# An audio tower's split into high and low halves: the fp16 high part written by ScalarE's second gelu pass instead of VectorE's cast

## The reference, cut to what matters

```python
CONV_LAYERS = [(128, 10, 5), (128, 3, 2), (128, 3, 2), (128, 3, 2), (128, 3, 2), (128, 2, 2)]
def _block(x, cw, cb, gw, gb, stride):
    y = lax.conv_general_dilated(x, cw, (stride,), 'VALID', ...) + cb[None, :, None]
    yg = y.reshape(B, NUM_GROUPS, C // NUM_GROUPS * T)
    mu, var = yg.mean(axis=-1, keepdims=True), yg.var(axis=-1, keepdims=True)
    yn = ((yg - mu) * lax.rsqrt(var + EPS)).reshape(B, C, T)
    return jax.nn.gelu(yn * gw[None, :, None] + gb[None, :, None])
h = x[:, None, :]
for (cw, cb, gw, gb), (_, _, s) in zip(conv_params, CONV_LAYERS):
    h = _block(h, cw, cb, gw, gb, s)
```

## Time and profile before

| what | us |
|---|---|
| median of 3 runs (from 1814.69 to 1819.27) | 1816.24 |
| the profiled execution | 1816.93 |
| its span, first to last instruction | 1815.3 |
| busy: TensorE matmuls, weight loads | 1464.7, 1019.8 |
| busy: VectorE, ScalarE, GpSimd | 1034.3, 754.8, 348.8 |
| mean granted clock of TensorE | 0.892 of full |

### The profile page before, as it was taken

How to read it: one execution, slowest core, us unless ns; L and a number is a source line. 1 busy time by engine, 2 the same in 40 slices (tenths; PEclk the granted TensorE clock), 3 DMA queues, 4 the chain that set the end, 5 groups by cost and what they waited for, 6 DMA issues and landing times.

```text
span 1815.3 us, 32241 instructions
## 1 busy us (share of the span) xinstructions
PE 1464.7 (81%) x10013; PEld 1019.8 (56%) x10014; DVE 1034.3 (57%) x2346; ACT 754.8 (42%) x1456; POOL 348.8 (19%) x390
## 2 busy tenths in 40 slices
PE   4975699998864899989747999898559999159997
PEld 3433477784433677753325777743347778137775
DVE  5987445558884445578964545598744546212221
ACT  2654355525642455435624555265435552012231
POOL 2000134300001334100002333000013331512111
PEclk7987699998986999989878999899769999579999
DMA  4300121210000221110002121100024332621110
GB/s 104 112 1 1 35 60 43 59 36 12 1 1 5 64 59 43 35 38 1 1 1 59 44 59 43 39 1 1 1 57 108 85 86 69 209 56 47 48 50 17
DMA packets 105852, 81.31 MB, mean 45 GB/s; under 512 B 57842, under 2 KB 96267, under 8 KB 105747
## 3 DMA queue, kind: packets, MB, share of 16 engines
q1 hardware_dynamic: 99988, 70.65, 15.5%
q0 software_dynamic: 5760, 9.36, 1.7%
HBM read 34.66 MB, written 18.38 MB: 29 GB/s over the span
## 4 chain that ended last, share of the span: by engine, by line
issue 50%; PE 30%; POOL 7%; DMA 4%; SPq 3%; DVE 3%; ACT 2%; POOLq 0%; DVEq 0%; ACTq 0%
PE ps L1649 5%; PE ps L1591 5%; PE ps L1802 4%; DMA arena<-arena 3%; PE ps L1635 3%; PE ps L1623 3%; PE ps L1782 2%; PE ps L1783 2%; POOL arena L765 2%; PE ps L1598 1%; POOL slot_scratch L824 1%; POOL arena L767 1%; SPq L587 1%; ACT arena L911 1%; PE ps L1790 1%
## 5 line engine op out<-in xcount | busy, mean ns | idle before, releaser
L1695 PE MATMUL ps<-arena,cwt 128*128 128x504 f16 (+2 forms) x1776 | 396.3, 387 | 62.1 <-DVE arena L1154 61.8
L1695 PEld LDWEIGHTS ps<-arena,cwt 128*128 128x128 f16 x1776 | 181.1, 104 | 268.3 <-DVE arena L1154 69.2
L1176 DVE TENSOR_REDUCE nmax<-ps 128x1 f32<-128x128 f32 (+5 forms) x288 | 176.9, 614 | 195.7 <-PE ps L1626 195.7
L1649 PE MATMUL ps<-arena 128*128 128x64 f32 (+2 forms) x2016 | 260.1, 269 | 9.1 <-DVE arena L1184 5.0
L1649 PEld LDWEIGHTS ps<-arena 128*128 128x128 f32 (+2 forms) x2016 | 241.9, 189 | 26.0 <-issue 17.8
L1156 DVE TENSOR_TENSOR arena<-arena 128x1008 f16<-128x1008 f32 (+4 forms) x200 | 227.0, 1135 | 6.9
L1184 DVE COPY arena<-ps 128x512 f32<-128x512 f32 (+4 forms) x288 | 156.1, 542 | 85.8 <-PE ps L1635 81.4
L893 ACT ACTIVATE arena<-ps,nmax 128x128 f32<-128x128 f32 (+5 forms) x288 | 180.8, 628 | 44.1 <-DVE nmax L1176 43.3
L1623 PE MATMUL ps<-arena 128*128 128x512 f16 (+6 forms) x780 | 164.6, 314 | 42.4 <-DMA arena<-arena 21.5
L1635 PE MATMUL ps<-ident,arena 128*128 128x128 f32 (+2 forms) x1008 | 165.8, 282 | 10.6 <-ACT arena L934 5.7
L950 ACT ACTIVATE arena<-ps 128x1008 f32<-128x1008 f32 (+1 forms) x112 | 96.3, 867 | 179.4 <-PE ps L1695 179.4
(11 more groups left out here) (249 smaller groups left out, 2060.5 us busy)
## 6 DMA issues: line engine op xcount, KB each, us to landing
arena<-arena SPq DMA_DIRECT2D x96, 187.5 KB, 3.0
arena<-arena SPq DMA_DIRECT2D x96, 93.8 KB, 2.6
slot_scratch<-empty_slot SPq DMA_DIRECT2D x1, 5775.0 KB, 19.1
arena<-in_L_ffn_w SPq DMA_DIRECT2D x8, 576.0 KB
arena<-in_L_ffn_w SPq DMA_DIRECT2D x8, 384.0 KB
arena<-slot_scratch SPq DMA_DIRECT2D x31, 96.5 KB, 1.9
arena<-slot_scratch SPq DMA_DIRECT2D x31, 96.0 KB, 2.0
xa<-in_x POOLq DMA_DIRECT2D x5, 468.8 KB, 4.3
```

The source lines that it names most:

```text
L1176: v.reduce_max(nmax[0:m, k_:k_ + 1], slot(g)[0:m, 0:128 * i + m], AX.X, negate=True).then_inc(S["smax_done"], 1)
L1649: last = t.matmul(slot(g)[0:m, Z_AT:Z_AT + DH], probt[k % 2][0:kk, c, 0:m], vt[0:kk, c, DH * hh:DH * hh + DH], start=c == 0, stop=c == i)
L1695: last = t.matmul(bank(g, k)[:, 0:c * PITCH].rearrange("p (r c) -> p r c", c=PITCH), cwt[layer][:, w, tap, :], parts[x][:, f:f + 2 * c - 1 ...
```

## The change

ScalarE makes the high part itself. For each piece of layer 0 and each chunk of layers 1 to 4 it now runs the gelu twice on the same source: first with the fp16 high part as its destination, then as before, to float32. VectorE's cast goes; it waits for ScalarE's `hi_done` and only subtracts. For a piece ScalarE waits for the low part only of the piece four earlier. Layer 5 has no split and stays. At the end of each batch ScalarE runs the tower's gelu on one column of ones.

```diff
-                for rows in NORM_CHUNKS[layer]:
+                for piece, rows in enumerate(NORM_CHUNKS[layer]):
...
+                    else:
+                        a.activation(split_views(layer, piece)[1], src, ACT.Gelu_apprx_tanh, bias=affine[:, 1:2],
+                                     scale=affine[:, 0:1]).then_inc(S["hi_done"], 1)
                     a.activation(dst, src, ACT.Gelu_apprx_tanh, bias=affine[:, 1:2], scale=affine[:, 0:1]
                                  ).then_inc(S["norm_done"], 1)
...
-                            wait(act, "hi_done", TOWER, SPLITS.index(had_it) + 1, b)
                             wait(act, "lo_done", TOWER, SPLITS.index(had_it) + 1, b)
                         src = slot(g).rearrange("p (m n) -> p m n", m=2)[:, :, 0:4 * PITCH]
+                        a.activation(split_views(0, piece)[1], src.rearrange("p m (k c) -> p m k c", c=PITCH),
+                                     ACT.Gelu_apprx_tanh, bias=affine[:, 1:2], scale=affine[:, 0:1]
+                                     ).then_inc(S["hi_done"], 1)
                         a.activation(stage[:, piece % STAGES, :].rearrange("p (m n) -> p m n", m=2), src,
...
+                a.activation(spare[:, 30:31], ones_col[:, :], ACT.Gelu_apprx_tanh)
...
-                n = SPLITS.index(unit) + 1
-                v.tensor_copy(high, src).then_inc(S["hi_done"], 1)
-                dve.wait_ge(S["hi_done"], at("hi_done", TOWER, n, b))
+                dve.wait_ge(S["hi_done"], at("hi_done", TOWER, SPLITS.index(unit) + 1, b))
                 v.tensor_tensor(low, src, high, ALU.subtract).then_inc(S["lo_done"], 1)
```

## The result

The changed kernel took 1913.66 us (median of 4 runs, 1913.17 to 1914.6) against 1815.92 for the kernel before beside it: 1.0536 times as long, 95% interval 1.0518 to 1.0554. The forecast was 1902, with a range from 1870 to 1932. The profiled execution took 1914.6 us, span 1912.6.

The account below looks back on a forecast made before the run. TensorE was taken to set the pace in the first two layers, with VectorE nearly full; later stages end with the last statistic. The parts sum to +21.4 us a batch, 85.6 in four, giving 1902 us, range 1870 to 1932.

Parts of the forecast that it names:

- Part one: First two layers, run together: second passes make ScalarE the bound instead of TensorE; +6.5 us a batch.
- The bound: First two layers: ScalarE replaces TensorE as the bound, and the 24 casts leaving VectorE give nothing.
- The price of the pass: Each added fp16 gelu of 1008 columns costs the same as the fp32 one: 1.08 us from PSUM, 1.12 from SBUF.
- part two: Layer 1 into 2: 26 passes leave TensorE without slots for 9.7 us, plus 1.9 us lost clock; +10.4 us a batch.
- Rival (b), the gate: First two layers: TensorE's short waits bring its clock to the lower level; +41 us a batch, 2066 us, chance 0.06.
- Parts three to five: Layers 2 into 3, 3 into 4 and 4 into 5: +3.3, +1.3 and -0.1 us a batch.
- Part six: Dummy gelu at batch end: its table load falls in idle time, the loop-head load stays; no cost, no gain.
- Rival (c): Faster if second passes, mainly layer 1 into 2, were hidden, costing at most 0.18 us each: 1796 us, chance 0.02.

Follow-up runs that it names:

- Layer 0 alone: Changed kernel with only layer 0's 24 pieces getting their high part from ScalarE, the rest cast by VectorE, without stating a gain: 1858.25 us, ratio 1.0213.
- layers 1 to 4 alone: Changed kernel with only layers 1 to 4 getting their high part from ScalarE, layer 0 cast by VectorE: 1874.02 us, ratio 1.0297.
- the run with filled waits: Changed kernel plus six thrown-away matmuls ahead of the waiting job in three of layer 0's eight groups: 1905.18 us, ratio 1.0468.
- The two runs with evictions between the passes: Changed kernel with five of layer 2's evictions among ScalarE's gelus: 1905.19 us; the same with four jobs' statistics among VectorE's splits: 1899.61 us.
- the touch alone: Kernel before with only the dummy gelu on a column of ones at each batch's end: 1819.46 us, ratio 1.000.
- the five chunks and every third piece: Kernel before, ScalarE making high parts of five layer 1 chunks and every third layer 0 piece, two evictions moved between gelus: 1805.6 us, ratio 0.9936.
- each set alone: Kernel before with only the five layer 1 chunks and two moved evictions: 1817.3 us; with only every third layer 0 piece: 1816.57 us.
- these mixes: Four variants of the kernel before with only some high parts made by ScalarE: 1817.3, 1805.6, 1804.87 and 1816.57 us.
- the first mix: Kernel before with ScalarE making high parts of five late layer 1 chunks, two evictions moved between its gelus: 1817.3 us, ratio 0.9999.

## Why the prediction was right, and where it was off

The time came 12 us above the forecast and inside the range. The mechanism of the sum is the one that the runs show, with one part missing: the lost clock in the first stage, which stood only among the rivals. Part one alone fell short by 13.8 us over the four batches; the other differences are small and of both signs.

- **The bound.** Right: ScalarE is the bound of the first stage (61.50 busy of 63.00 us) and of the stage behind it, and the casts that left VectorE gave nothing back. Layer 0 alone and layers 1 to 4 alone show both halves.
- **The price of the pass.** Right: from PSUM a pass comes every 1.08 us, from SBUF every 1.12, with fp16 as with fp32.
- **Part one was mis-sized**: +6.5 us forecast, +9.54 measured in batch 2, 9.3 to 11.6 in all. It had no term for lost clock in this stage, though part two had one for its gap. TensorE meets slot waits of 1.56 us, and the spells of low clock behind them are the larger piece of the error: the run with filled waits gives back 8.6 us of the 13.8 that are missing, and shows 76.3 to 76.5 us for the stage, +7.8 over 68.6. The 1.3 us that are left for each batch are in batch 2 of that run, in three small pieces: the last piece is through 60.35 us behind the load's end where 59.7 were worked out, the way from there to TensorE's end is 9.24 us for 9.0, and from there to the next GpSimd operation it is 4.37 us where it was 3.98.
- **Rival (b), the gate**, had been given 0.06 as an all or nothing. It came true in part: the waits were longer than the "pieces under 1 us" that the prediction argued from, and the attention's short gaps were no argument about 1.56 us. The low clock came for 3.4 us at a time, behind five of twelve waits, not for the stage.
- **Part two.** Right in size (+10.60 for 10.4) and in the order of its steps: 27.5 us for the passes, a hole of 9.38 us for 9.7, and 11.94 us for the 45 matmuls where 9.4 + 1.9 = 11.3 were said. The half clock lasted 4.5 us, not the 3.5 to 4 that were read from the earlier trace rows, where finer windows give 3.3; the errors of this part partly cancel. The two runs with evictions between the passes add what was not said: the order of VectorE's queue stands right behind, so filling the hole alone would have given 2 us.
- **Parts three to five.** Right within 0.4 us in every batch; in batch 2 +2.96, +1.36 and -0.16 us. Two of the terms were rounded up beyond their own working: the copies came 15.6 - 12.5 = 3.1 us later for the 3.3 that were taken, and 1.1 for the 1.3 of layer 3 into 4, so that the second fits as well as it does is in part luck.
- **Part six.** Right: 1.000 for the touch alone, and the load at the head of the loop is in the trace.
- **Rival (c)** did not come true, and no run tests its bound of 0.18 us for a second pass, but it points to what works: a pass by ScalarE is free only where another engine sets the pace and ScalarE has a gap, as the five chunks and every third piece have together; each set alone gained nothing that can be told. The expectations for these mixes were too high by 5 to 13 us, in part because they let the clock of the stages behind stand as it was, in part because the stages that were changed gained less than was worked out (1.5 us for 3 in the first mix).

What stays open: what sets the moment at which the clock changes. A low spell follows the same wait of 1.56 us in five cases of twelve and not in the others, and the half clock at a stage's start lasts 3.3 us in one kernel and 5.7 in another whose work there is the same. No run here separates the causes.

## What to carry to other kernels

A pass that moves from a busy engine to an idle one has to be placed in the receiver's queue: ask what stands behind it there (here the evictions that free PSUM), and move only as many passes as fit where the receiver waits anyway; 13 of the 50 gained 0.6%, all 50 lost 5.4%. When the new bound makes TensorE wait in the middle of dense work, count the wait and a possible spell of half clock behind it as separate terms. And where short stages follow each other, judge a gain in one by the whole chain, since a shifted start can hand part of it back as clock.

## What the runs showed of the hardware

- More matmuls made a kernel faster: 72 thrown away in the waits took 8.6 us off the four first stages.
- In an unbroken row of passes from PSUM the duration shown for one grows from 1.19 to 1.27 us and more and falls back to 1.19 after a pause, while their starts stay 1.08 us apart. The mean of 1242 ns in the lines by form is therefore no slower pass.
- A table that is loaded already is loaded again: 1.28 us at the end of the batch and 1.28 us at its head.
- A spell of low clock in the middle of dense matmuls lasted 3.4 us and added 1.7 us to them, each time; which of the equal waits it follows changed from kernel to kernel and from batch to batch.
- No drain shows at the load: in the kernel before the first pass starts 0.02 us behind its end, with the touch 0.01 us. At the end of a batch of the kernel after the load starts 0.02 us behind the last instruction before it.
